# Summing 23 instead of 15 middle tables in a recommendation tower, with a scratch of their own for the shelf numbers, gathers queued without ring waits, and every engine's order rewritten

## The reference

```python
e = jnp.stack([tbl_0[ids[:, 0]], tbl_1[ids[:, 1]], ..., tbl_38[ids[:, 38]]], axis=1)   # 2048 x 39 x 64
s = jnp.sum(e, axis=-1)                       # 2048 x 39
z = s[:, _ROW] * s[:, _COL]                   # 2048 x 741, all pairs
h = jnp.concatenate([z, dense_ctx], axis=1)
h = jnp.maximum(h @ W_top1 + b_top1, 0.0)
h = jnp.maximum(h @ W_top2 + b_top2, 0.0)
y = h @ W_top3
```

## Time and profile before

| what | value |
|---|---|
| median of 3 runs | 198.47 us |
| the profiled execution, first to last instruction | 314.8 us |
| PE, DVE, POOL, ACT busy in it | 207.8, 144.2, 114.8, 81.2 us |
| bytes moved by DMA | 43.70 MB |
| gathers on POOL | 116 |

### The profile page before, as it was taken

The page is one execution under the profiler, slowest core; times in us unless marked ns, Lnnn a source line. Parts: engine busy times, 40 slices in busy tenths (PEclk is TensorE's granted clock), DMA queues, the critical chain, the costliest instruction groups (busy, mean ns, idle before and its releaser), DMA issues.

```text
span 314.8 us, 4373 instructions
## 1 busy us (share of the span) xinstructions
PE 207.8 (66%) x1659; PEld 126.9 (40%) x1659; DVE 144.2 (46%) x384; ACT 81.2 (26%) x144; POOL 114.8 (36%) x124
## 2 busy tenths in 40 slices
PE   0652102499794321118956988856999999999996
PEld 0310000344131100004613655653566776667784
DVE  2000000157990000002964679561589988968440
ACT  0200010268980000000064224210132424035432
POOL 6777777000077777740473320537310000000000
PEclk9955555589667555555985999977599999999999
DMA  7811131189924132115693676999124029100000
GB/s 290 286 29 30 27 93 25 46 300 413 418 87 129 25 69 89 25 21 186 221 342 121 217 254 218 350 351 244 25 60 150 2 77 275 52 2 2 2 0 0
DMA packets 13557, 43.70 MB, mean 139 GB/s; under 512 B 3216, under 2 KB 4256, under 8 KB 13408
## 3 DMA queue, kind: packets, MB, share of 16 engines
q1 hardware_dynamic: 9392, 39.42, 36.1%
q0 software_dynamic: 3712, 3.81, 5.8%
q10 hardware_dynamic: 432, 0.19, 0.2%
HBM read 43.14 MB, written 0.27 MB: 138 GB/s over the span
## 4 chain that ended last, share of the span: by engine, by line
PE 51%; issue 31%; DVE 7%; ACT 5%; another core or an unknown queue 3%; DMA 2%; ACTq 0%; DVEq 0%
PE g L1119 8%; PE ph L1226 8%; PE ph L1227 7%; PE ph L1230 6%; PE ph L1119 5%; PE s L1205 3%; DVE mid_sums L505 2%; PE g L1165 2%; PE g L1102 2%; PE ph L1246 2%; PE g L1140 2%; DMA stage<-early 2%; PE ph L1250 2%; PE ph L1247 2%
## 5 line engine op out<-in xcount | busy, mean ns | idle before, releaser
L429 POOL DMA_INDIRECT rows<-tab,idc x68 | 65.8, 968 | 77.9 <-DVE w_lo L522 32.8
L438 POOL DMA_INDIRECT rows<-tab,idc x48 | 46.4, 968 | 36.7 <-DVE bsum L587 18.4
L1119 PE MATMUL g<-stage,fc 128*32 128x100 f32 x378 | 27.3, 318 | 41.2 <-issue 40.2
L1119 PE MATMUL ph<-stage,fc 128*32 128x96 f32 (+2 forms) x378 | 20.9, 285 | 39.9 <-issue 30.6
L1226 PE MATMUL ph<-z_hi,w_hi 126*128 126x512 f32 (+1 forms) x96 | 44.8, 467 | 0.0
L536 DVE TENSOR_SCALAR hots<-hots,fc 125x2048 bf16<-125x2048 bf16 x28 | 20.7, 751 | 43.6 <-issue 42.5
L1227 PE MATMUL ph<-z_hi,w_lo 126*128 126x512 f32 (+1 forms) x96 | 39.7, 413 | 0.7 <-issue 0.7
L1230 PE MATMUL ph<-z_lo,w_hi 126*128 126x512 f32 (+1 forms) x96 | 39.3, 409 | 0.0
L1119 PEld LDWEIGHTS g<-stage,fc 128*32 128x32 f32 x378 | 15.8, 139 | 52.6 <-issue 50.9
L1119 PEld LDWEIGHTS ph<-stage,fc 128*32 128x32 f32 x378 | 12.4, 134 | 49.1 <-issue 47.9
L478 DVE CAST mparts<-g 125x100 bf16<-125x100 f32 x3 | 0.8, 262 | 62.4 <-PE g L1119 50.4
(11 more groups left out here) (88 smaller groups left out, 269.0 us busy)
## 6 DMA issues: line engine op xcount, KB each, us to landing
stage<-middle SPq DMA_DIRECT2D x17, 800.0 KB
hots<-shelf_scratch SPq DMA_DIRECT2D x17, 512.0 KB
stage<-early SPq DMA_DIRECT2D x3, 768.0 KB
stage<-middle SPq DMA_DIRECT2D x3, 750.0 KB
stage<-early SPq DMA_DIRECT2D x3, 640.0 KB
rows<-tab,idc POOLq DMA_INDIRECT x116
slot_b<-slot_scratch SPq DMA_DIRECT2D x8, 224.0 KB
stage<-early SPq DMA_DIRECT2D x3, 512.0 KB
```

The lines of the kernel that those rows point to most:

```text
L429: pool.indirect_dma_start(rows[:, n % ROW_RING, i, :], None, gathered[i], bass.IndirectOffsetOnAxis(ap=idc[:, n, i:i + 1], axis=0)).then_i ...
L438: pool.indirect_dma_start(rows[:, n % ROW_RING, i, :], None, gathered[i], bass.IndirectOffsetOnAxis(ap=idc[:, n, i:i + 1], axis=0)).then_i ...
L1119: mm = pe.matmul(bank[j * LANE:(j + 1) * LANE, 0:w], band, stage[:, q, (r * 4 + j) * w:(r * 4 + j + 1) * w], start=(x == 0), stop=(x == PA ...
```

## The change

1. `SUMMED` becomes (3, 6, 7, 7): 23 chunk-fields are summed, 9 are gathered. Gathers fall from 116 to 84 (36 of the middle tables, 48 of the large), and seven middle tables are loaded instead of five. Tables 1 and 3 are still summed by DVE, 0, 2, 4, 5 and 6 by PE.
2. The middle shelf numbers get input rows, two DVE operations (`mid_shelves`), a DRAM scratch and one broadcast DMA for each chunk; the five spreads on PE and five copies on ACT for them go.
3. The ring of `rows` is replaced by a buffer for each of two middle chunks (`rows_m`) and one of 16 tiles for the large fields (`rows_l`). Gathers are issued in a new order, large fields first in chunk 0, and only the middle ones of chunks 2 and 3 wait for sums.
4. A lookup of six or seven fields is done in two parts (`LOOK_PARTS`). The weights land in other borrowed buffers and are loaded right behind the first early tables.
5. The lists of all engines are new.

```diff
-SUMMED = (1, 4, 5, 5)
+SUMMED = (3, 6, 7, 7)
...
+LOOK_PARTS = [[(0, n)] if n <= LOOK_MAX else [(0, (n + 1) // 2), ((n + 1) // 2, n)] for n in SUMMED]
...
-        rows = sb("rows", [P, ROW_RING, NL, DIM], F32)
-        asum = sb("asum", [P, TILES, NA], F32)
+        rows_two = [sb(f"rows_m{c}", [P, TILES, NA - SUMMED[c], DIM], F32) if SUMMED[c] < NA else None for c in (0, 1)]
+        rows_m = [rows_two[c % 2][:, :, 0:NA - SUMMED[c], :] if SUMMED[c] < NA else None for c in range(CHUNKS)]
+        rows_l = sb("rows_l", [P, ROW_RING, NB, DIM], F32)
+        asum = sb("asum", [P, 2, TILES, NA], F32)
...
             def load_mid_shelves(c):
...
-                n = min(SUMMED[c], 4)
-                sp.dma_start(mid_hots[:, 0:n, :],
-                             shelf_dram[c:c + 1, NE:NE + n, :]
-                             .rearrange("c f n -> c (f n)").partition_broadcast(P)).then_inc(mid_hots_in, 16)
+                sp.dma_start(mid_hots[:, 0:SUMMED[c], :],
+                             mid_dram[c * NA:c * NA + SUMMED[c], :].rearrange("(o f) n -> o (f n)", o=1)
+                             .partition_broadcast(P)).then_inc(mid_hots_in, 16)
...
+            def fetch_a(c, a, b):
+                if c == 1:
+                    pool.wait_ge(w1_split, KCH)
+                elif c >= 2:
+                    pool.wait_ge(a_summed, (c - 1) * TILES)
...
+            def fetch_b(c, a, b):
                 if c >= 2:
-                    pool.wait_ge(b_summed, n - ROW_RING + 1)
+                    pool.wait_ge(w1_split, 5)
...
+            def mid_shelves():
+                dve.wait_ge(mid_idr_in, 16)
+                dve.tensor_scalar(mid_shelf_f, mid_idr, 1.0 / WMID, 0.5 / WMID - 0.5, ALU.mult,
+                                  ALU.add).then_inc(mid_shelf_calc, 1)
+                dve.wait_ge(mid_shelf_calc, 1)
+                dve.tensor_scalar(mid_shelf_h[:, :], mid_shelf_f, ROUND, ROUND, ALU.add,
+                                  ALU.subtract).then_inc(mid_shelf_calc, 1)
...
+            mid_look(1, 3, 3, 6, G1)
+            pe.wait_ge(mid_picked_ready, 33)
+            mid_sum(6, 0, G0)
+            mid_sum(6, 1, G0)
+            mid_sum(6, 2, G0)
             sel(1, 2)
+            mid_sum(6, 3, G0)
+            pe.wait_ge(mid_picked_ready, 36)
+            turn_a(1, G1)
             L1(1, 0, 0)
             L1(1, 0, 1)
```

More of the change, by code:

```diff
@@ L587, in sum_b @@
-                dve.tensor_reduce(bsum[:, t, 0:NB], rows[:, slot, NA:, :], AX.X, ALU.add).then_inc(b_summed, 1)
+                n = c * TILES + t
+                dve.wait_ge(rows_b_in[n], 16 * NB)
+                dve.tensor_reduce(bsum[:, c % 2, t, 0:NB], rows_l[:, n % ROW_RING, :, :], AX.X, ALU.add).then_inc(b_summed, 1)
             def split_a(c):
                 dve.wait_ge(cleared, 1)
-                dve.wait_ge(a_summed, (c + 1) * TILES)
+                if SUMMED[c] < NA:
+                    dve.wait_ge(a_summed, sum(SUMMED[x] < NA for x in range(c + 1)) * TILES)
@@ L631, in _ @@
             mid_ids()
+            sum_b(0, 0)
             ids()
+            split_dense()
+            split_w2()
+            mid_shelves()
+            split_tables(0)
+            split_w1(0)
+            split_w1(1)
+            sum_b(0, 1)
+            split_w1(2)
+            split_w1(3)
+            split_w1(4)
             hot(0, 0)
-            split_tables(0)
-            pick(0, 0, G1)
-            sum_a(0, 0)
-            hot(0, 1)
+            split_w1(5)
+            pick(0, 0, G0)
@@ L702, in _ @@
+            mid_pick(0, 2, 0, 3, G1, 3)
+            dve.wait_ge(mid_picked_ready, 6)
+            mid_pick(0, 3, 0, 3, G0, 4)
+            pick(1, 1, G1)
+            sum_a(0, 3)
+            row_sum(3, 0, 1)
+            split_a(0)
+            row_sum(3, 1, 0)
+            row_sum(3, 1, 1)
+            row_sum(3, 2, 0)
             multiply(0, 3)
+            row_sum(3, 2, 1)
+            z_low(0, 3)
+            mid_hot(1)
+            sum_b(1, 0)
             multiply(0, 4)
-            hot(1, 4)
```

1108 lines of the change are left out of this document (573 added, 535 removed).

## The result

| | before | changed |
|---|---|---|
| median of the runs, us | 198.47 (198.32 to 199.13) | 222.92 (221.23 to 224.93) |
| ratio to before, 95% interval | | 1.118 (1.106 to 1.130) |
| span of the recorded execution shown here, us | 198.5 (recorded again) | 219.3 |
| bytes, gathers | 43.70 MB, 116 | 50.95 MB, 84 |

It is slower, as forecast, but by 24.5 us and not 6.5, and outside the range. The changed kernel's profile shows no crawl (long stretches of single small matmuls with pauses), so it can't be laid beside the one of the earlier trace rows.

The account below looks back on a forecast made before the run. The prediction took loads as the bound until table 6 arrives, then PE: 107 us for table 6, 1 for its last piece's sums, 97 for the rest, 205 us in all; range 190 to 213.

Parts of the forecast that it names:

- The crawl belongs to the profiled execution only: PE's slow stretches at 0:60.4 and 98:144, 116 us of the profile, were taken as absent from an ordinary run.
- Gathers are no bound: POOL's gathers, 1.27 us each, were taken to have 17 to 21 us of slack, so fewer gain nothing.
- A gather is 0.25 us longer beside a compare of 0.75: A POOL gather under a DVE one-hot compare was read as taking 1.19 instead of 0.94 us.
- Without the crawl this ends at 45.6 us: Chunk 0's ACT-bound stretch of 31.6 us was put after a start of 14 us in an ordinary run.
- -2 for ACT: Weights' copies moved to where ACT waits for the first tables: up to -4 us or nothing, taken as -2.
- Before: 83, well below 106, so there the loads had room: Loads ahead of table 4's last piece were priced at 83 us of full queues, against its sums ending near 106.
- Table 6 in at 107: Loads would bring in table 6, the last middle table, at 102 to 113 us; 107 was taken.
- DVE's floor for the same point, 99, is covered by it: DVE's floor up to the last table was 14 + 31.6 - 2 + 5 + 50 = 99 us, below the loads' 107.
- The rest behind the last table, 97: PE's work from the last table's sums to the end would grow from 92 to 97 us.
- Third rival, 216: Broadcasts waiting for lookups in SP's list hold table pieces, then PE, 3 us each time: 216 us; chance 0.07.

Follow-up runs that it names:

- before, again: The kernel before the change, unedited, recorded a second time; time 200.3 us, span 198.5 us.
- e_summed_1455: Changed kernel with the old table numbers (1, 4, 5, 5), without the sums, lookups and loads of tables 5 and 6; 214.1 us, ratio 1.093.
- e_mid0_late: Changed kernel with PE's sums of middle table 0 moved back behind the last early lookup, four chunk 1 slot spreads moving back too; 233.9 us, ratio 1.175.
- e_both_late: Changed kernel with the weights loaded behind the early tables and table 0's sums moved back behind the last early lookup; 236.0 us, ratio 1.194.
- b_extra_bytes: Kernel before the change with eight added copies of 0.8 MB between its loads, read by nobody; 214.3 us, ratio 1.072.
- e_tables1to6_small: Changed kernel with pieces of tables 1 to 6, except piece 3 of table 1, loading 64 columns, 18 MB less; 218.7 us, ratio 1.118.

## Why the prediction was wrong, step by step

- *The crawl belongs to the profiled execution only*: right, shown by the second recording.
- *Gathers are no bound*: right. Before, again, has no wait for gathered rows. `e_summed_1455` has as many gathers as before, and (3, 6, 7, 7), which takes 32 away, makes the span 7.5 us longer still.
- *A gather is 0.25 us longer beside a compare of 0.75*: this holds for that row, where the gather began first. In before, again, a gather that begins under a compare is longer by nearly all that is left of it:

```profile
14.19 0.76 DVE L536 TENSOR_SCALAR hots<-hots,fc 125x2048 bf16<-125x2048 bf16 x1 [5.93 <-ACT hots L876]
14.37 1.39 POOL L429 DMA_INDIRECT rows<-tab,idc  x1 [0.30 <-issue]
```

Here 0.58 us of the compare are left and the gather takes 1.39 instead of 0.94. The forecast doesn't hang on it.
- *"Without the crawl this ends at 45.6 us", then -2 for ACT*: this step failed. I let the weights move "to where ACT waits for the first tables" and counted a gain of 2. The first phase grew by 10.1. I had read the lists around the last middle table and not the first ten entries of each, where three waits for late data had been put ahead of the shelf numbers, the first sum and the first copy. My own reading said that ACT bounds chunk 0, so a later first copy of ACT had to be counted in full. 5.8 us of the 10.1 stand in the two timelines of the start; that a late start is handed on about one for one was shown in the kernel before; up to 3.7 may come from the sums of table 0 and the slot spreads between the lookups, by `e_mid0_late`, though `e_both_late` did not keep that gain. Which wait costs how much is open.
- *"Before: 83, well below 106, so there the loads had room"*: wrong. In the first 106.3 us of before, again, q1 moved 31.65 MB at 79.1% and the gathers took 8.5%, so the engines were busy for some 94 us. The price was too low: 0.376 MB for each us of full queue and not 0.406. And what was idle was no room, as `b_extra_bytes` showed.
- *Table 6 in at 107*: it came at 119.2, and I named it "the term that decides". Both fail. Up to 119.2 us q1 moved 41.0 MB at 92.1%, 0.373 MB for each us, less than my 0.406 for tables. But without 18 MB (`e_tables1to6_small`) PE came to the last sum of table 6 at 120.4 all the same. Two chains end there together, and the order of the engines is the firm one.
- *"DVE's floor for the same point, 99, is covered by it"*: this is the second step that failed. The chain of the engines' own work and waits, which I had put at 99, reaches this point at about 120 with hardly any bytes of tables, 21 us later. I had added busy times of one engine for each stretch and no waits between engines.
- *The rest behind the last table, 97*: 99.2 from its sums to the end. The PE work that I counted is there (+6.7 busy against +5.3), and DVE waits 4.1 us for the slots, which I had not counted. That 97 and 99.2 lie so close is partly luck, since the forecast had no such wait. `e_summed_1455`, without the added tables, has 3.3 us more than before behind the last cut.
- *Third rival, 216*: nearest in time, but its mechanism, table pieces held behind broadcasts, is not what cost: PE waited for pieces of middle tables 2.3 us in all and DVE 0.9, and with 18 MB less the first three phases stay as long.

In sum: of 20.8 us of span 13.3 come with the change without its added tables (10.2 in front), and 7.5 with the tables; by the ratios it is about four fifths and one fifth. Bytes of the tables cost up to 4.8 us in the last phase. The new lists are the likely cause of the larger part, but `e_summed_1455` also keeps the other buffers, the scratch and the earlier weights, and which of them costs what was not separated.

## What to carry over

When lists are rewritten, read the first entries of every engine before anything else: a wait there for late data can delay the engine that bounds the first stage, and where several stand side by side, as here, removing one may gain nothing. Adding up busy times gives a floor, and here the waits between engines put 20 us on it. Measure how full a queue is in an ordinary execution, and whether its idle time is room: only added bytes showed it. Here a broadcast that landed late behind full queues was not helped by another queue, while fewer bytes helped.
